# A hybrid attention and mixture-of-experts layer on one core: routing of the second expert pass in four equal parts, two more shared blocks behind the first pass's routed blocks, and half of the index tables made by ScalarE

## What is computed

```python
x = L0_attn_a_x                                   # 16 x 256 tokens of 128 features
x = x + attn_a(layernorm(x), W_q, W_k, W_v)       # global mean of K*V, times Q
x = x + ffn(layernorm(x), ...)                    # first expert pass
x = x + attn_b(layernorm(x), qkv_w, ...)          # softmax attention, 16 heads of 8
x = x + ffn(layernorm(x), ...)                    # second expert pass, same weights

def ffn(x, ...):                                  # 8 experts, the best 2 for each token
    p = softmax(x @ gate_w + gate_b)
    v, i = top_k(p, 2); v = v / (sum(v) + 1e-9)
    w = sum(one_hot(i) * v)
    y_e = gelu(x @ ew1[e] + eb1[e]) @ ew2[e] + eb2[e]
    return x + mlp(x, shared weights) + sum_e w[e] * y_e
```

## Time and profile before

| | |
|---|---|
| median of 3 runs | 807.68 us (806.96 to 810.85) |
| the profiled execution | 808.51 us |
| its span, first to last instruction | 806.7 us |
| mean granted TensorE clock | 0.924 of full speed |
| busy share of the span | PE 82%, DVE 78%, ACT 65%, POOL 62% |
| the chain of work that ended last | PE 52%, DVE 26%, ACT 9%, issue 5%, POOL 3%, DMA 2% |

### The profile page before, as it was taken

One profiled execution on the slowest core, in us unless ns is written; L12 is line 12 of the kernel. 1 busy time (PEld: TensorE's weight loads), 2 busy tenths in 40 slices (PEclk: granted clock), 3 DMA queues, 4 the chain that ended last, 5 costly groups with the idle time before them and its releaser, 6 DMA issues.

```text
span 806.7 us, 22802 instructions
## 1 busy us (share of the span) xinstructions
PE 664.0 (82%) x7807; PEld 478.8 (59%) x7808; DVE 628.6 (78%) x1404; ACT 524.2 (65%) x1256; POOL 497.2 (62%) x512
## 2 busy tenths in 40 slices
PE   0565399699999946898988899999978999999990
PEld 0343389588988943343433444444437988988990
DVE  6699969487777636999999999789856448878748
ACT  4666754276666634588888888778965656666740
POOL 4997516678887068668248837106877717777750
PEclk9999589799999985699999999889997999999995
DMA  7232210133334411001000100000111323232227
GB/s 206 69 89 33 78 29 1 28 79 91 86 83 80 65 43 40 24 8 41 9 2 13 40 5 1 2 2 15 40 57 53 112 53 91 80 83 84 81 78 250
DMA packets 52521, 46.88 MB, mean 58 GB/s; under 512 B 8787, under 2 KB 44795, under 8 KB 52456
## 3 DMA queue, kind: packets, MB, share of 16 engines
q1 hardware_dynamic: 43368, 28.02, 12.4%
q0 software_dynamic: 9088, 17.98, 9.1%
HBM read 26.76 MB, written 20.13 MB: 58 GB/s over the span
## 4 chain that ended last, share of the span: by engine, by line
PE 52%; DVE 26%; ACT 9%; issue 5%; POOL 3%; DMA 2%; SPq 1%; DVEq 0%; POOLq 0%; ACTq 0%
PE ps L931 25%; PE ps L1075 12%; DVE mx L2374 10%; PE ps L1090 5%; PE ps L1326 4%; PE ps L1167 2%; DVE xres L2250 2%; POOL ytok L880 2%; ACT scratch L1664 2%; ACT xn L1459 2%; PE ps L1339 1%; DVE hlo L2367 1%; DVE hhi L2361 1%; DVE stats L1766 1%; DVE rnorm L1820 1%
## 5 line engine op out<-in xcount | busy, mean ns | idle before, releaser
L1546 ACT ACTIVATE h<-ps,b1T 128x256 f32<-128x256 f32 x440 | 171.8, 479 | 58.5 <-PE ps L931 54.9
L2374 DVE TENSOR_REDUCE mx<-ps 128x2 f32<-128x512 f32 x256 | 171.4, 684 | 17.6 <-PE ps L931 16.5
L1664 ACT ACTIVATE scratch<-ps 128x512 f32<-128x512 f32 x256 | 152.9, 616 | 36.3 <-PE ps L931 34.5
L931 PE MATMUL ps<-xg,w1s 128*128 128x256 f16 x936 | 117.3, 276 | 11.6 <-issue 10.0
L1075 PE MATMUL ps<-w2s,hhi 128*128 x1248 | 117.3, 219 | 0.0
L880 POOL DMA_INDIRECT ytok<-yst,didx x78 | 89.4, 1146 | 44.0 <-DVE yst L2184 23.0
L931 PE MATMUL ps<-kst,qst 32*128 32x256 f16 x512 | 98.5, 288 | 18.0 <-DVE mx L2374 14.3
L770 POOL DMA_INDIRECT scratch<-rows,tok_i x78 | 91.6, 1175 | 26.8 <-issue 20.4
L931 PEld LDWEIGHTS ps<-xg,w1s 128*128 x936 | 88.1, 99 | 25.8 <-issue 15.4
L1572 ACT ACTIVATE xg<-ps 128x512 f16<-128x512 f16 x78 | 46.5, 597 | 82.1 <-PE ps L1167 82.0
L2124 DVE SCALAR_TENSOR_TENSOR hlo<-h,hhi 128x1024 f16<-128x1024 f32 x78 | 95.6, 1225 | 2.7
(11 more groups left out here) (318 smaller groups left out, 1377.9 us busy)
## 6 DMA issues: line engine op xcount, KB each, us to landing
gy<-rows SPq DMA_DIRECT2D x39, 136.0 KB, 2.2
ysorted<-yst SPq DMA_DIRECT2D x39, 128.0 KB, 1.8
h<-in_L_ffn_ew SPq DMA_DIRECT2D x16, 256.0 KB, 3.1
scratch<-ytok SPq DMA_DIRECT2D x16, 256.0 KB, 3.6
xres<-in_L_attn_a_x SPq DMA_DIRECT2D x4, 512.0 KB, 5.5
rows<-hl SPq DMA_DIRECT2D x4, 512.0 KB, 3.1
out_x<-xres SPq DMA_DIRECT2D x3, 512.0 KB, 4.6
scratch<-rows,tok_i POOLq DMA_INDIRECT x78
```

Of the source, the lines that this page charges most:

```text
L931: return pe.matmul(o, a, b, start=start, stop=stop)
L1546: last = act.activation(h32[:, u % 2, f], HB[u % 2][:, f], ACT.Gelu_apprx_tanh, bias=b1T[:, ds(e * CH + c, 1)], scale=1.0 / PS)
L1664: act.activation(prb[:, (s // 4 * 4 + (s + 2) % 4) % 8, :], ps[:, s % 2, :], ACT.Exp, scale=HD ** -0.5 / (PS * PS))\
L2374: dve.tensor_reduce(mx[:, c, j:j + 5:4], ps[:, 2 + s % 2, :].rearrange("p (n k) -> p n k", n=2), AX_X, ALU.max).then_inc(Att.mx, 1)
```

## The change

AHEAD replaces SA: the first pass runs 10 shared blocks ahead and 6 in the ramp, the second pass 12 and 4 as before. In the first pass PE counts after the first shared block instead of after the second, the eight `number` groups stand two to a shared block at blocks 3 to 7, ACT multiplies `oneblk` by the token numbers (four activations for a group), and the turn of routed block 0 stands ahead of the last shared block. `norm(1)` deals its rows out otherwise between DVE and ACT. POOL's adding of `xn` leaves `norm(1)` and stands, a pair of tiles at a time, behind the gathers of the routed blocks 8 to 23.

The second pass has four parts of eight tiles: the first is chosen at bodies 9 and 10, the second at bodies 11 and 12, the third at body 15, the fourth after the attention. POOL makes the sums and slots of the first two.

```diff
-    SA = NS - 4
+    AHEAD = (10, NS - 4)
-    PARTS = ((0, 2 * GT), (2 * GT, GT), (3 * GT, GT))
+    PARTS = tuple((GT * g, GT) for g in range(NG))
...
-        POSTS = {7: {6: ("P", 0), 11: ("P", 1)}, 8: {6: ("P", 2), 11: ("P", 3)},
-                 11: {0: ("P", 4), 6: ("P", 5), 8: ("P", 6), 11: ("P", 7), 13: ("gate", 7)}, 12: {8: ("rank", 0)},
-                 14: {6: ("P", 8), 8: ("P", 9), 11: ("P", 10), 12: ("P", 11), 15: ("gate", 11)}, 15: {9: ("rank", 1)}}
+        POSTS = {7: {6: ("P", 0), 11: ("P", 1)}, 8: {6: ("P", 2), 11: ("P", 3), 13: ("gate", 3)},
+                 10: {8: ("rank", 0)}, 11: {0: ("P", 4), 6: ("P", 5), 8: ("P", 6), 11: ("P", 7), 13: ("gate", 7)}, 12: {8: ("rank", 1)},
+                 14: {6: ("P", 8), 8: ("P", 9), 11: ("P", 10), 12: ("P", 11), 15: ("gate", 11)}, 15: {9: ("rank", 2)}}
...
             def moe_rows():
...
-                for g in range(NG):
-                    pool.wait_ge(l.hi, NG + g + 1)
-                    pool.tensor_tensor(group(xres, g), group(xres, g), group(xn, g), ALU.add).then_inc(l.added, 1)
...
-                with pool.Fori(0, T // 8) as i:
-                    for u in range(2):
-                        g = 2 * i + u
-                        pool.wait_ge(m.inblk, g + 1)
-                        ids = ids16[:, ds(4 * g, 4)].unsqueeze(2).unsqueeze(2).to_broadcast([P, 4, TOPK, NT])
-                        pool.tensor_tensor(oneblk[:, u, :, :, :], oneblk[:, u, :, :, :], ids, ALU.mult)\
-                            .then_inc(m.numbered, 1)
...
                 for f in range(NBLK):
                     fetch_rows(f)
+                    if 8 <= f < 8 + NBATCH:
+                        b = f - 8
+                        pool.wait_ge(m.y, 2 + m.ahead)
+                        pool.tensor_tensor(two(xres, b), two(xres, b), two(xn, b), ALU.add).then_inc(l.added, 1)
...
-            sum_first()
-            place_first()
-            post_send(0, GT // 4)
+            sum_part(0)
+            place_part(0)
+            post_send(0, GT)
+            sum_part(1)
+            place_part(1)
+            post_send(GT, GT + GT // 2)
             post_rows(2)
-            post_send(GT // 4, GT // 2)
+            post_send(GT + GT // 2, 2 * GT)
             post_lo(2)
-            post_send(GT // 2, GT)
-            for g in range(1, NG):
+            for g in range(2, NG):
                 post_send(GT * g, GT * (g + 1))
...
+                def number(g):
+                    act.wait_ge(m.inblk, g + 1)
+                    for c in range(4):
+                        last = act.activation(oneblk[:, g % 2, c, :, :], oneblk[:, g % 2, c, :, :], ACT.Copy,
+                                              scale=ids_c[:, 4 * g + c:4 * g + c + 1])
+                    last.then_inc(m.numbered, 1)
+
+                def inverse_beside_shared():
+                    tables = {4: (0,), 5: (1, 2), 6: (3,), 7: (4, 5), 8: (6, 7)}
+                    for n in range(m.ahead):
+                        for g in tables.get(n, ()):
+                            number(g)
+                        gelu_shared(n)
...
+                    p = {9: 0, 10: 0, 11: 1, 12: 1}.get(b)
+                    if p is not None and (b, s) in ((9, 14), (11, 14)):
+                        dve.wait_ge(Post.gate, GB * (p + 1))
+                        Route.top(p, part_of(glog, p))
```

More of the change, by code:

```diff
@@ L1105, in moe_blocks, with turn @@
                 pe.wait_ge(ewt_used, NE)
+                def turn(n, u, i):
+                    if r == 0:
+                        pe.wait_ge(m.gath[u], 16 * BT * (i + 1))
+                    else:
+                        pe.wait_ge(Post.load[u], 16 * (i + 1))
+                    for h in range(2):
+                        for t in range(BT):
+                            o = h * BR + t * P
+                            f = slice(h * D, (h + 1) * D)
+                            last = pe.transpose(TB[u % 2][:, o:o + P],
+                                                grow[:, BT * u + t, f] if r == 0 else erow[:, u, t, f], ident16[:, :])
+                    last.then_inc(m.turn, 1)
                 def inverse_beside_shared():
@@ L1142, in last_group_beside_shared @@
                     down_shared(2)
-                    for n in range(3, SA):
+                    for n in range(3, m.ahead):
                         down_shared(n)
-                        if n + 2 < SA:
+                        if n + 2 < m.ahead:
                             up_shared(n + 2)
@@ L1192, in moe_blocks @@
                     else:
-                        up_shared(SA + u - 1)
+                        up_shared(m.ahead + u - 1)
                     down_routed(NBLK - 3 + u, u, es[u])
-                for n in range(SA, NS):
+                for n in range(m.ahead, NS):
                     down_shared(n)
@@ L1796, in norm_rows @@
                                                         ALU.subtract, ALU.mult)
-                    last.then_inc(l.norm, 1)
+                    return last
                 def lo(g):
@@ L2050, in post_last, with shared_result @@
                 post_add(g)
+            def shared_result(r, n):
+                m = moe[r]
+                q = turn_of(m, n)
+                if r == 1:
+                    dve.wait_ge(Post.added, n // GB + 1)
+                elif n >= m.ahead:
+                    dve.wait_ge(Ln.added, n + 1)
+                dve.wait_ge(m.down, q + 1)
+                o = two(xres, n)
+                dve.scalar_tensor_tensor(o, YB[q % 2], 1.0 / WS, o, ALU.mult, ALU.add).then_inc(m.y, 1)
             def moe_blocks(r):
@@ L2154, in invert @@
                     dve.tensor_scalar(tok_i[:, :], IDX, float(MIDDLE), None, ALU.add).then_inc(m.tok, 1)
-                    for n in range(2 + T // 4, SA):
+                    for n in range(7, m.ahead):
                         result_shared(n)
@@ L2275, in moe_blocks @@
                     scattered()
-                    for n in range(SA, NS - 2):
+                    for n in range(m.ahead, NS - 2):
                         result_shared(n)
@@ new lines, in attn_body @@
+                    if p is not None and (b, s) in ((9, 15), (11, 15)):
+                        Route.lower(p, part_of(glog, p))
+                        Route.tied(p)
+                    if p is not None and b in (10, 12):
+                        if s == 0:
+                            Route.lowest(p, 0)
+                            Route.choose(p, 0)
+                        if s == 1:
+                            Route.without(p)
+                            Route.top_left(p)
+                        if s == 2:
+                            Route.equal(p)
+                        if s == 4:
+                            Route.numbered(p)
+                            Route.lowest(p, 1)
+                        if s == 6:
+                            Route.choose(p, 1)
+                            Route.both(p)
@@ L2459, in attn_body @@
                     if (b, s) == (15, 2):
                         dve.wait_ge(Post.gate, 3 * GB)
-                        Route.first(1, part_of(glog, 1))
+                        Route.first(2, part_of(glog, 2))
                     if (b, s) == (15, 4):
-                        Route.second(1)
+                        Route.second(2)
                     if (b, s) == (15, 6):
-                        Route.third(1)
-                    if body.post(s, "rank") and b == 15:
+                        Route.third(2)
```

287 lines of the change are left out of this document (145 added, 142 removed).

## The result

The changed kernel takes 827.74 us (median of 826.28, 830.51, 815.7 and 829.19) beside 809.26 for the kernel before (median of 807.68, 806.96, 810.85 and 811.07): a ratio of 1.017, 95% interval 1.011 to 1.023. The forecast was 812.3 with a range to 820, so the loss is real, and three to four times as large as the sum had it (+13.5 us by the ratio and +18.5 by the medians, for +4.6). The profiled execution took 826.28 us; its span is 824.5 us, 17.8 more than before, and its mean granted clock 0.916 for 0.924.

The account below looks back on a forecast made before the run. PE was taken to bound the routed blocks, DVE and PE level in the attention. Terms -12.2 + 7.5 + 0 + 9.3 = +4.6 us on 808.5 gave 813.1, 812.3 as a median, range 798 to 820.

Parts of the forecast that it names:

- the clock behind the stop at body 14: Attention: after PE's stop its clock falls, costing 2 us, from 0 to 4.
- `post_lo(2)` late by eight sends: Attention, POOL's queue: eight more sends, 10.1 us, stand ahead of `post_lo(2)`, which ends at 581.0 instead of 574.6.
- PE's wait: Attention, body 14: PE reaches its turn of batch 8 at 575.4 and waits 5.6 us for `post_lo(2)`.
- own-time sum of 813.1: Whole kernel: the terms' total of +4.6 us added to the profiled execution's 808.5 us.
- Tables, norm and start, -12.2: First pass up to the routed blocks: 9.3 us gained by tables, 0.8 by `norm(1)`, 2.1 at the routed blocks' start.
- Loop, +7.5: First pass's routed blocks: POOL's additions among the gathers make sixteen blocks 3.60 us instead of 3.03, losing 7.5, from 0 to 14.
- the lead: Routed blocks: gathers run 3.7 us ahead of PE, its earlier start takes 2.1, and 1.6 is left against the 9.1 loss.
- Ramp, 0: Between routed blocks and attention: two more shared blocks fit into PE's idle 10.8 us; cost 0, from -1.5 to 1.
- Attention without the stop, +1.8: Attention: choosing experts in smaller parts costs DVE 1.8 us more, all of which counts.
- Second pass, 0: Second pass's start: the last send comes earlier but already had 7 us to spare, so nothing changes.
- The likeliest case: First rival: both queues wait, in the loop and at body 14, 812.3 us, own range 807 to 818; chance 0.40.
- the third rival: The loop loses 7.5 us but `post_lo(2)` comes in time, as if bodies 12 and 13 were longer: 804.8; chance 0.13.

Follow-up runs that it names:

- the filled stop: Changed kernel with 26 matmuls of zeros (5.5 us) ahead of PE's wait for `post_lo(2)` at body 14: 816.14 us, ratio 1.009.
- the late low half: Kernel before, with eight POOL sends ahead of `post_rows(2)` and eight between it and `post_lo(2)`, instead of four and four: 818.21 us, and 938.26 on a slow chip.
- the kernel with both edits: Changed kernel with POOL's sixteen additions behind the last gather and `post_lo(2)` four sends behind `post_rows(2)`, the other eight sends after it: 797.24 us, ratio 0.988.
- low-half-early kernel: Changed kernel with four sends of part 1, `post_rows(2)`, four sends, `post_lo(2)`, then the other eight sends: 805.17 us, ratio 0.998.

## Why the prediction was wrong

**The failed step is a term of the sum, the clock behind the stop at body 14: "I take 2 us, from 0 to 4". It measured 12.7 us by the filled stop**, more than three times its upper bound. Everything before it in that paragraph held: `post_lo(2)` late by eight sends, PE's wait (5.6 forecast, 5.57 and 5.4 measured), the idle ACT and DVE behind it, the lower clock. The price came from the earlier trace rows, misread: a granted clock of 0.86 over 50 us is two times 6.8 us of half clock, and not 0.14 of the 50. The 7 steps lost in them are 7.1 us, so the 2 us of the sum stand for some 4 us of half clock at that price. How long the clock stays down was not asked. Here it was down for 20.5 us and 13.7 more, in the second profile 37.5 us in one piece, with PE busy 90% of the first stretch and 99% of the second. With 12.7 in place of 2.0 the own-time sum of 813.1 becomes 823.8, beside 826.3 measured. In the kernel before a stop of 6.4 us was followed by 17.1 us of half clock only, and cost 11.2 us with the stop itself; that the clock's part of it is some 5 is a difference and was not measured, since that kernel with a filled stop ran only on a chip on which PE never stood. From body 14 to the second pass's routed blocks the changed kernel has 47.8 us of half clock and 10.2 with the stop filled, and the kernel before 27.3 with the late low half and 13.7 without. So a microsecond of half clock cost about a third of one in both (12.7 of 37.6 and 4.8 of 13.6, an estimate from these differences). Why the changed kernel's clock stays down longer is open. (The prediction's wait is 5.6 us where it is worked out and 5.5 in its sum, which changes nothing.)

**Tables, norm and start, -12.2: measured -12.1 at `hhi` 0, though by other shares.** Tables -10.7 for -9.3, since an activation costs 0.33 and not 0.39. Norm nothing: `mask` starts at 110.15 as it did at 110.12. The start -1.3 for -2.1.

**Loop, +7.5: measured +10.2 and, between the two kernels of one chip that differ in the additions alone, 10.9 (7.9 as medians).** The mechanism is the one described, and the pace was right: `hhi` 8 to 24 takes 57.3 us for 48.7, 3.58 a block for the 3.60 of the sum. But the lead did not save 1.6 us, and the 14 blocks behind, which the sum had at nothing, take 44.1 for 42.5. PE's new waits from 160 to 262 us are 5.3 us for the gathers and 2.8 for ACT's `h`. Missing was that DVE waits too: `hlo` and `hhi` have means of 1342 and 796 ns from 169 to 219 us, where the kernel with both edits has 1225 and 694. What of the loop's loss is theirs is not shown. The Trainium skill, SBUF — State Buffer, section "SBUF: two separate sides", says that of two contenders for the shared ports whichever starts first keeps them for its whole instruction. The addition at 200.41 agrees: it began 0.08 us into an `hhi` of 0.75, took 1.24 for 0.74 and ended 0.57 behind it. The `hlo` of 2.06 us does not decide it, as it is recorded as begun 0.23 us before the addition, which was not lengthened, and the gather ahead of that ran until 195.53. That a gather might pass `hlo`, as the prediction weighed, did not happen: the one issued 0.39 us into `hlo` at 198.35 took 1.66 and ended 0.83 behind it.

**Ramp, 0: -0.7.** The two shared blocks fit into it.

**Attention without the stop, +1.8: between 0 and 3.8.** The low-half-early kernel takes 239.0 us from body 0 to 14 as the kernel before does, but with 16.5 us of half clock for 23.4; the changed one takes 242.1 with 23.5, and 242.8 and 242.2 in the other profiles. They part around body 7 to 8, where the first has 3.4 us of half clock at 438.5 and the others 10.2 from about 440 or 444, though their instructions are the same up to there. Bodies 8 to 10, at full clock in both, take the low-half-early kernel 2.1 us more than the kernel before, near the 1.8. Bodies 11 and 12 take it 3.4 less, with 3.4 us of half clock for 13.6; how much of that is the smaller parts' is not shown.

**Second pass, 0: 0.** The last send was 9.5 us ahead of PE's last shared block.

**The likeliest case was the right one**: both queues wait, though at a price outside its own range of 807 to 818. The rivals fell on chips of 808 us. On those of 923 to 940 us the third rival, "`post_lo(2)` comes in time", is what happens.

The best kernel keeps the change and takes out its two prices: additions behind the gathers and the low half ahead of the sends, 797.24 beside 807.41 us. It does not collect all of it: it is 15.9 us ahead of the kernel before at body 0, and its attention up to body 14 then takes 9.5 us more, with 40 us of half clock where the kernel before has 23. Why is open; this one profile lies 4.8 us above the median of its runs.

## What to carry to other kernels

Price a stop of TensorE in a full stretch in two parts, the stop and the clock after it. Behind the stop of 5.6 us the second was 12.7 us, found by giving PE idle work for just the wait; behind that of 6.4 us it was about 5, by difference. When work is added to a queue, look for the one late thing in it that another engine needs and place that first; what only has to be done some time goes behind it. A queue that keeps pace with the bound has no room: 0.73 us of additions in each of sixteen blocks of 3.03 cost the loop 10 to 11 us, and behind the last gather they delayed nothing.

## What the runs showed of the hardware

The half clock outlasts its cause: behind the stop PE was busy 34.25 of 37.5 us in the second profile of the changed kernel, and 13.54 of 13.70 us from 603.3 in the first, at half clock all the way.

```profile
579.50:617.00 37.50, 34.25 (x277) 0.50 0.03 9
```

Chips differ by 16% on the same kernel (807 and 940 us). More half clock explains under half of it: with the late low half the kernel before has 256 us of it on the one and 148 on the other and is 118 us longer, and 108 us at half speed can cost PE at most 54 (an estimate from these two traces). In the second pass, at a clock of 0.97, the time from the first to the last `hhi` is 135.6 us instead of 114.1, and PE waits there for ACT's copies, which it does not in the kernel before on its chip. The 135.6 us and this row are of the kernel before with the late low half, the row from 790 to 900 us:

```profile
PE ps L930 <- ACT xg L1571: 10.1, 8, 2.6
```

What holds up ACT there no run here shows. A change that costs 1.2% on one chip (the late low half) costs nothing on the other.
